# The order of the opening rearranged, and transposed probabilities as the weights of the value products

## The reference, cut to what matters

```python
def _L0_xattn_ref(q, k, v, mask, Wq, Wk, Wv, Wo):      # q = layernorm(x), k = v = ctx
    scores = jnp.einsum('bhqd,bhkd->bhqk', qh, kh) / scale
    scores = jnp.where(mask, NEG_INF, scores)
    attn = jax.nn.softmax(scores, axis=-1)
    ctx = jnp.einsum('bhqk,bhkd->bhqd', attn, vh)      # the value products
    return ctx.transpose(0, 2, 1, 3).reshape(B, S, D) @ Wo.T
x = x + _L0_xattn_ref(...)
# _L0_ffn_ref: logits -> top_k(2) -> softmax of the two = weights of the two experts
x = x + _L0_ffn_ref(_layernorm(x), ...)
```

## Time and profile before

| | |
|---|---|
| median of 3 runs | 192.21 us |
| the profiled execution | 192.32 us |
| its span | 190.5 us |
| granted clock of TensorE, mean | 0.991 of full |
| busy shares: TensorE, VectorE, ScalarE, GpSimd | 91%, 85%, 68%, 47% |

### The profile page before, as it was taken

One profiled execution on the slowest core, in us unless ns is written; L12 is line 12 of the kernel. 1 busy time (PEld: TensorE's weight loads), 2 busy tenths in 40 slices (PEclk: granted clock), 3 DMA queues, 4 the chain that ended last, 5 costly groups with the idle time before them and its releaser, 6 DMA issues.

```text
span 190.5 us, 4273 instructions
## 1 busy us (share of the span) xinstructions
PE 173.7 (91%) x1305; PEld 125.4 (66%) x1305; DVE 161.5 (85%) x505; ACT 129.8 (68%) x288; POOL 89.4 (47%) x146
## 2 busy tenths in 40 slices
PE   7888888879699999999899889999999999999962
PEld 7763555445556666666658566778887887887841
DVE  5577989999689998999994799987989798989981
ACT  3195897778569989999788855566555656565641
POOL 7059993595968888888778790500000000000000
PEclk9999999999889999999999999999999999999999
DMA  5999100000000000000000533232345235323301
GB/s 112 305 326 392 60 2 2 3 0 0 5 0 2 3 0 0 0 0 3 2 0 19 170 105 110 110 126 92 122 122 173 80 128 167 115 90 121 116 2 55
DMA packets 12128, 15.43 MB, mean 81 GB/s; under 512 B 1744, under 2 KB 6608, under 8 KB 11984
## 3 DMA queue, kind: packets, MB, share of 16 engines
q1 hardware_dynamic: 10800, 13.79, 22.1%
q10 hardware_dynamic: 1312, 1.46, 2.8%
HBM read 14.06 MB, written 1.18 MB: 80 GB/s over the span
## 4 chain that ended last, share of the span: by engine, by line
PE 53%; DVE 19%; POOL 7%; issue 7%; ACT 6%; DMA 4%; ACTq 1%; DVEq 0%; POOLq 0%
PE bank L1093 30%; PE bank L1040 8%; PE bank L1031 4%; DMA mhalf<-mask_half 4%; PE bank L1022 4%; DVE hid L905 4%; DVE smax L828 4%; DVE prob L849 3%; POOL k_blk L453 3%; ACT hid_hi L660 2%; PE bank L1011 2%; PE bank L1001 2%; POOL rstd L427 1%; DVE hid_lo L897 1%; PE bank L991 1%
## 5 line engine op out<-in xcount | busy, mean ns | idle before, releaser
L1040 PE MATMUL bank<-k_blk,q_blk 128*128 128x512 f32 x64 | 34.8, 629 | 1.1 <-POOL k_blk L453 0.9
L651 ACT ACTIVATE sig<-bank 128x512 f32<-128x512 f32 x36 | 21.5, 599 | 19.6 <-PE bank L1093 18.5
L453 POOL TENSOR_TENSOR k_blk<-k_all,consts_sb 128x512 f32<-128x512 f32 x32 | 33.1, 1056 | 0.0
L660 ACT CAST hid_hi<-hid 128x512 fp32r<-128x512 f32 (+1 forms) x37 | 22.4, 608 | 11.4 <-DVE hid L905 11.3
L1093 PE MATMUL bank<-xt_hi,w_hi 128*128 (+1 forms) x72 | 29.2, 406 | 0.2 <-ACT sig L651 0.2
L1093 PE MATMUL bank<-xt_hi,w_lo 128*128 (+1 forms) x72 | 28.3, 393 | 0.0
L1093 PE MATMUL bank<-xt_lo,w_hi 128*128 (+1 forms) x72 | 28.2, 392 | 0.0
L897 DVE TENSOR_TENSOR hid_lo<-hid,hid_hi 128x512 fp32r<-128x512 f32 (+1 forms) x37 | 25.1, 679 | 3.7 <-ACT hid_hi L660 3.3
L600 ACT ACTIVATE prob<-prob,exp_scale 128x512 f32<-128x512 f32 x32 | 23.8, 743 | 2.5 <-DVE prob L849 2.5
L888 DVE TENSOR_TENSOR hid_u<-sig,bank 128x512 f32<-128x512 f32 x32 | 21.8, 682 | 4.1 <-PE bank L1093 2.5
L828 DVE TENSOR_REDUCE smax<-bank 128x8 f32<-128x512 f32 x32 | 21.9, 684 | 2.8 <-PE bank L1040 2.8
(11 more groups left out here) (117 smaller groups left out, 333.7 us busy)
## 6 DMA issues: line engine op xcount, KB each, us to landing
cb<-comb_rows SPq DMA_DIRECT2D x64, 128.0 KB, 2.9
w_moe_sb<-w_moe SPq DMA_DIRECT2D x1, 1296.0 KB, 10.7
ctxt_sb<-ctx_t SPq DMA_DIRECT2D x4, 256.0 KB, 8.7
xt_sb<-x_t ACTq DMA_DIRECT2D x4, 256.0 KB, 7.7
x_sb<-x SPq DMA_DIRECT2D x4, 256.0 KB, 10.3
out<-x_sb SPq DMA_DIRECT2D x3, 256.0 KB, 3.1
w_moe_sb<-w_moe SPq DMA_DIRECT2D x1, 432.0 KB, 8.0
w_att_sb<-w_att SPq DMA_DIRECT2D x1, 264.0 KB, 4.7
```

Of the source, the lines that this page charges most:

```text
L453: last = nc.gpsimd.tensor_tensor(k_blk[p][:, g, :, :], k_all[:, bass.ds(t, 1), g, :].broadcast_to([P, HG, S]), hmask_sb.rearrange("p (h o) ...
L651: nc.scalar.activation(sig[r][:, :], gate_ps[r][:, :], ACT.Silu).then_inc(s_sig, 1)
L660: nc.scalar.copy(hid_hi[k][:, cols], hid[k][:, cols]).then_inc(s_hid_hi, 1)
L1040: nc.tensor.matmul(score_ps[g][:, :], q_blk[q][:, g, :, :].rearrange("p b s -> p (b s)"), k_blk[q][:, g, :, :].rearrange("p h s -> p (h s) ...
```

## The change

1. The probabilities become the weights: each of the 16 products of a tile loads 128 keys by 64 queries of `prob_t` as weights and moves 18 columns of `v_blk`. Batch `b` of every pair stands in the strip of columns `64 * b`, so there are two strips of 64 columns in place of four of 32. The output has queries on partitions, so `values_as_rows`, the copy to `pvt_sb` and their semaphores go, and VectorE reads the products' own output. `v_blk` shrinks from 32 to 18 columns for a pair, and the two memsets that zeroed its rest go. The copy that fills `v_blk` gets a wait for the products that read the buffer before.
2. VectorE's `norm1(1)` moves ahead of step -1, `keys(2)` from step 0 to step -1, `norm1(2)` from step 1 to step 0, `keys(3)` from step 2 to step 1, `norm1(3)` from step 3 to step 2. GpSimd's `rstd1_of(2)` moves from step 2 to step 1, `rstd1_of(3)` from step 3 to step 2.
3. The two operations of `weights_of_two` move from VectorE to ScalarE, behind the tanh.

```diff
@@ -121,8 +120,7 @@
 
         q_blk = [sb(f"q_blk{p}", [P, 2, BPT, S]) for p in range(2)]
         k_blk = [sb(f"k_blk{p}", [P, 2, HG, S]) for p in range(2)]
-        v_blk = [sb(f"v_blk{p}", [P, BPT, PAIRS, PW]) for p in range(2)]
-        pvt_sb = sb("pvt_sb", [P, 2 * P])
+        v_blk = [sb(f"v_blk{p}", [P, BPT, PAIRS, 2 * DV]) for p in range(2)]
         smax = [sb(f"smax{p}", [P, HEADS]) for p in range(2)]
         prob = [sb(f"prob{p}", [P, HEADS * S]) for p in range(2)]
         prob_t = [sb(f"prob_t{p}", [P, PAIRS, P]) for p in range(2)]
@@ -269,8 +265,7 @@
 
         score_ps = banks[5:7]
         pt_ps = [banks[7], banks[0]]
-        pvt_ps = banks[1][:, 0:2 * P]
-        pv_ps = banks[1][:, 2 * P:]
+        pv_ps = banks[1][:, 0:PAIRS * 2 * DV]
         at_ps, wo_ps, tail_ps = (bank[:, 0:P] for bank in banks[2:5])
 
         gate_ps = [banks[5], banks[7]]
@@ -346,6 +341,7 @@
 
             tiles = slice(half * TILES // 2, (half + 1) * TILES // 2)
             eng.wait_ge(s_w_top, half + 1)
+            eng.wait_ge(s_marked, half + 1)
             for k, dst in ((0, comb[half]), (1, comb_b[half])):
                 last = ops.tensor_tensor(dst[:, :, :], dst[:, :, :],
                                          w_top[:, tiles, k].rearrange("p (o t) -> p o t", o=1)
@@ -413,9 +409,6 @@
             nc.gpsimd.memset(neg_half[:, :], -0.5).then_inc(s_half, 1)
             nc.gpsimd.memset(eps_sb[:, :], LN_EPS).then_inc(s_half, 1)
             nc.gpsimd.memset(neg_mean_sb[:, :], -1.0 / D).then_inc(s_half, 1)
-            for p in range(2):
-                nc.gpsimd.memset(v_blk[p][:, :, :, :].rearrange("p b j w -> p (b j w)"), 0.0).then_inc(s_vwide, 1)
-
             nc.gpsimd.memset(v_all[:, TILES // 2:, :, :, :, :].rearrange("p t b j e d -> p (t b j e d)"), 0.0)\
                 .then_inc(s_zero[1], 1)
             pool.wait_ge(s_half, 4)
@@ -494,8 +487,8 @@
                     nc.gpsimd.tensor_tensor(bias2[p][:, :], neg_mean2[p][:, :], rstd2[p][:, :], ALU.mult).then_inc(s_bias2, 1)
                 if on(-2):
                     k_blocks(t + 2, p)
-                    if isinstance(t, int) and t in (0, 2, TRAIL):
-                        rstd1_of(1 + (t + 1) // 2)
+                    if isinstance(t, int) and t < GROUPS - 1:
+                        rstd1_of(t + 1)
                     if isinstance(t, int) and t == TRAIL:
                         pool.wait_ge(s_q_sb, GROUPS)
                         pool.wait_ge(s_k_sb, GROUPS)
@@ -576,13 +569,14 @@
                     act.wait_ge(s_wmoe[1], 16)
                 if on(-1):
                     if isinstance(t, int) and t < 0:
-                        act.wait_ge(s_vwide, 2)
                         act.wait_ge(s_vden, 2)
                         act.wait_ge(s_v_sb, 1)
                     elif isinstance(t, int) and t == 0:
                         act.wait_ge(s_v_sb, GROUPS)
 
-                    nc.scalar.copy(v_blk[q][:, :, :, 0:2 * DV].rearrange("p b j w -> p (b j) w"),
+                    if not (isinstance(t, int) and t < 1):
+                        act.wait_ge(s_pv, t)
+                    nc.scalar.copy(v_blk[q][:, :, :, :].rearrange("p b j w -> p (b j) w"),
                                    v_all[:, bass.ds(t + 1, 1), :, :, :, :].rearrange("p o b j e d -> p (o b j) (e d)"))\
                         .then_inc(s_vblk, 1)
                 if on(0):
@@ -618,9 +612,6 @@
                     nc.scalar.copy(xt2_hi[:, cols], tail_ps[:, 0:P]).then_inc(s_xt2_hi, 1)
                 if on(-1):
                     exponentials(0)
-                if on(0):
-                    act.wait_ge(s_pvt, t + 1)
-                    nc.scalar.copy(pvt_sb[:, :], pvt_ps).then_inc(s_pvt_sb, 1)
                 if on(-1):
                     exponentials(1)
 
@@ -633,6 +624,11 @@
                 tiles = slice(half * TILES // 2, (half + 1) * TILES // 2)
                 act.wait_ge(s_top_f, (half + 1) * TILES // 2)
                 nc.scalar.activation(half_tanh[:, tiles], gap[:, tiles], ACT.Tanh, scale=0.5).then_inc(s_tanh, 1)
+                act.wait_ge(s_tanh, half + 1)
+                for k, sign in ((0, -0.5), (1, 0.5)):
+                    last = nc.scalar.activation(w_top[:, tiles, k], half_tanh[:, tiles], ACT.Identity, scale=sign,
+                                                bias=half_sb[:, 0:1])
+                last.then_inc(s_w_top, 1)
 
             for g in range(GROUPS):
                 queries_out(g)
@@ -766,7 +762,6 @@
 
             def top_two(half):
                 experts_marked(half)
-                weights_of_two(half)
 
             def experts_marked(half):
 
@@ -775,17 +770,10 @@
                 iota_bc = iota_sb.rearrange("p (e o) -> p e o", o=1).broadcast_to(shape)
                 dve.wait_ge(s_top_f, (half + 1) * TILES // 2)
                 for k, dst in ((0, comb[half]), (1, comb_b[half])):
-                    nc.vector.tensor_tensor(dst[:, :, :], iota_bc,
-                                            top_f[:, tiles, k].rearrange("p (o t) -> p o t", o=1).broadcast_to(shape),
-                                            ALU.is_equal)
-
-            def weights_of_two(half):
-
-                tiles = slice(half * TILES // 2, (half + 1) * TILES // 2)
-                dve.wait_ge(s_tanh, half + 1)
-                for k, sign in ((0, -0.5), (1, 0.5)):
-                    last = nc.vector.tensor_scalar(w_top[:, tiles, k], half_tanh[:, tiles], sign, 0.5, ALU.mult, ALU.add)
-                last.then_inc(s_w_top, 1)
+                    last = nc.vector.tensor_tensor(
+                        dst[:, :, :], iota_bc, top_f[:, tiles, k].rearrange("p (o t) -> p o t", o=1).broadcast_to(shape),
+                        ALU.is_equal)
+                last.then_inc(s_marked, 1)
 
             def step(t, p, on):
                 q = 1 - p
@@ -832,7 +820,7 @@
                 if on(-1):
                     row_max(0)
                 if on(1):
-                    pv = pv_ps.rearrange("p (j w) -> p j w", w=PW)[:, :, 0:2 * DV].rearrange("p j (e d) -> p j e d", e=2)
+                    pv = pv_ps.rearrange("p (j e d) -> p j e d", e=2, d=DV)
                     dve.wait_ge(s_pv, t)
                     nc.vector.reciprocal(inv_den[q][:, :].rearrange("p (j e) -> p j e", e=2), pv[:, :, :, DK]).then_inc(s_iden, 1)
                     dve.wait_ge(s_iden, t)
@@ -853,16 +841,15 @@
                             ALU.subtract).then_inc(s_sub[g], 1)
                 if isinstance(t, int) and t == LEAD:
                     keys(1)
-                    norm1(1, 1)
-                if isinstance(t, int) and 0 <= t <= TRAIL:
-                    g = 2 + t // 2
-                    if t % 2 == 0:
-                        keys(g)
-                    else:
-                        norm1(g, g % 2)
+                    keys(2)
+                if isinstance(t, int) and t == 0:
+                    norm1(2, 0)
+                if isinstance(t, int) and t == 1:
+                    keys(3)
+                if isinstance(t, int) and t == 2:
+                    norm1(3, 1)
                 if isinstance(t, int) and t == TILES - 4:
                     experts_marked(0)
-                    weights_of_two(0)
                 if isinstance(t, int) and t == TILES - 3:
                     combined(dve, nc.vector, 0, s_route[0])
 
@@ -870,6 +857,7 @@
             share_rows(2)
             share_rows(3)
             norm1(0, 0)
+            norm1(1, 1)
             peel(step, LEAD)
             dve.wait_ge(s_bias, 16)
 
@@ -984,13 +972,6 @@
                     last = nc.tensor.matmul(v_ps[:, i * P:(i + 1) * P], ctxt_sb[:, c:c + P], wv_sb, start=True, stop=True)
                 last.then_inc(s_v, 1)
 
-            def values_as_rows(t):
-
-                pe.wait_ge(s_pvt_sb, t + 1)
-                for g in range(2):
-                    last = nc.tensor.transpose(pv_ps[:, g * P:(g + 1) * P], pvt_sb[:, g * P:(g + 1) * P], ident_sb)
-                last.then_inc(s_pv, 1)
-
             def attention_transposed(t, p):
                 pe.wait_ge(s_att, t + 1)
                 nc.tensor.transpose(at_ps, att[p][:, :, :].rearrange("p h d -> p (h d)"), ident_sb).then_inc(s_at, 1)
@@ -1029,8 +1010,10 @@
                         j = h * GT + c
                         for b in range(BPT):
                             last = nc.tensor.matmul(
-                                pvt_ps[c * PW:(c + 1) * PW, h * P + b * S:h * P + (b + 1) * S], v_blk[p][:, b, j, :],
-                                prob_t[p][:, j, b * S:(b + 1) * S], start=True, stop=True, tile_position=(0, c * PW))
+                                pv_ps[b * S:(b + 1) * S, j * 2 * DV:(j + 1) * 2 * DV],
+                                prob_t[p][:, j, b * S:(b + 1) * S],
+                                v_blk[p][:, b, j, :],
+                                start=True, stop=True)
                     return last
 
                 def scores(g):
@@ -1048,12 +1031,10 @@
                     pe.wait_ge(s_sub[0], TILES)
```

(13 more changed lines are left out.)

5 lines of the change are left out of this document (1 added, 4 removed).

## The result

| | before | changed |
|---|---|---|
| median, us | 191.87 (190.25 to 194.24, 20 runs) | 193.08 (191.73 to 196.15, 20 runs) |
| ratio to before | | 1.0066, 95% interval 1.0036 to 1.0096 |
| profiled execution, us (span) | 192.32 (190.5) | 196.15 (194.0) |
| mean granted clock, profiled | 0.991 | 0.970 |

The change makes the kernel slower by 0.7%. I had forecast 192.0 and no difference. The profiled execution of the changed kernel is its longest, and the ratio leaves out the five longest runs of the changed kernel and the three longest of the kernel before.

A forecast was written before the change was run, and what follows sets the result against it. Two tied circles bound a step at 4.52 us: TensorE's queue, and logits through `att` and value products to the router. Terms -2.0 + 2.2 - 0.45 - 0.1 = -0.35 against the profiled 192.32 gave 192.0 us, range 188.8 to 197.0.

The forecast's parts named there:

- The value products, +0.31 a tile: Value products on TensorE: weight loads bound them, 1.03 us a tile for 0.72, making loop steps 4.83 for 4.52.
- The sum over steps 5 to 11: Loop steps 5 to 11: seven circles, each longer by 0.31 us for the value products, +2.2 us.
- the rule that I had weighed: TensorE's value products: loads overlap running products only in other row groups; as a rival 194.2 us, chance 0.07.
- The opening, -2.0: Steps -1 to 4: moving norms and 1/sqrt earlier removes GpSimd's wait at the loop's entry, -2.0 us.
- 0.25 - (7.09 - 4.83): Opening: step 3 some 0.25 us later, step 4 falling from 7.09 to 4.83 if the clock stays; -2.0 us.
- Rival 1: Opening: half clock comes all the same, 193.4 us, chance 0.25; with an opening that gives nothing, 194.0, another 0.10.
- Step 12, -0.45: Step 12: VectorE loses the two weight operations to ScalarE, -0.45 us, between 0 and -0.57.
- costed the experts at nothing: Experts after the steps: TensorE's queue alone, unchanged; ScalarE's two operations, up to 0.2 us, paid by VectorE's freed 0.5.
- The end of the steps, -0.1: After the last step: without the `pvt_sb` copy ScalarE's table load starts earlier, part lost to lateness, -0.1 us.

The follow-up runs named there:

- the filled kernel: The changed kernel plus short products of constants in TensorE's waits of steps 2 and 3 and at the end: 191.82 us, ratio 1.0024 to before.
- `values_only`: The kernel before with only the change's value products, without `pvt_sb` and its transposes, old order kept: 194.11 us, ratio 1.0164.
- `wtop_only`: The kernel before with only the two operations on `w_top` moved to ScalarE: 190.83 us beside 190.78, ratio 0.9979.
- the filled kernels: Order alone, changed kernel and four strips, each with short constant products in TensorE's waits of steps 2 and 3 and at the end: 189.22, 191.82, 188.55 us.
- the order alone: The kernel before with everything of the change but the value products: 189.85 us, ratio 0.9925; with TensorE's waits filled 189.22.
- the four strips: The changed kernel with each value product cut in two, 32 queries as weights in four strips of 32 columns: 188.74 us, ratio 0.9878; filled 188.55.

## Why the prediction was wrong, point by point

**The value products, +0.31 a tile: right.** 1.04 forecast as 1.03, steps of 4.83, 0.52 of waiting, 0.2 us of idle TensorE ahead of the transpose of `att` (the second score product starts at 65.97 and takes 0.43, the transpose comes at 66.61). The sum over steps 5 to 11, forecast as +2.2, is 29.04 + 4.77 = 33.81 us now and 31.96 before, +1.9: step 7 had been 4.81 already. Loads 0.058 us apart in a strip with 64 columns go on beside that strip's products, as the trace has them. By the rule that I had weighed (the Trainium skill, TensorE: Matmul & The Clock Gate, Packing small matmuls), they would have waited for them, as the row group is the same; the measurement decides against it here.

**The opening, -2.0: this step failed**, in its term 0.25 - (7.09 - 4.83). The step of 4.83 came out where the clock stayed: 4.85 in the filled kernel, behind a step 3 of 6.05 for 5.91 (+0.14; 0.25 was forecast). What failed is the 7.09 and the condition "if the clock stays". At full clock the old order's step 4 is 5.92, with the new products in it (`values_only`), so the same term would have given 0.25 - (5.92 - 4.83) = -0.8; most of the rest of the -2.0 was clock. Without it the whole opening gains about 1.0: 34.28 us from the first row maximum to that of step 5, for an estimate of 35.3 (next paragraph).

The term added two things that do not belong together. One was real: the order shortens the way to step 5. With the new products on both sides and no half clock it is 34.28 us from the first row maximum to that of step 5 (filled) for 35.50 (`values_only`), -1.2. With the old products the changed order has 33.64 us (filled); for the old order no trace has it without half clock, and an estimate is 36.68 less the 1.4 that 3.41 us of half clock cost, 35.3: about -1.6. (The old order shows such a price too: `wtop_only`, with 3.41 us more of half clock than before, takes 1.46 us more over steps 3 to 5.) The other was the half clock itself. I read it in one profiled execution, called its disappearance a gain and set the sum against that execution. But it is not a property of the order. Of the kernel before, about half the runs have it: of the 17 beside the filled kernels 8 end between 190.3 and 191.0, with a mean clock of 0.998 to 1.00, and 9 between 191.4 and 193.0, with 0.988 to 0.993. The changed kernel has it more often: 17 of its 26 runs end above 192.5, and 13 have a mean clock of 0.978 or less, which 4 of the 51 runs of the kernel before beside the experiments have (part of that clock is lost at the end of the kernel). My 192.0 is in truth the time of the changed kernel where the clock stays: 191.82 with the waits filled.

**Rival 1 came true**, at the price given for it: "the clock falls in the opening all the same", 193.4, with 0.25. Measured 193.08. That the two agree to 0.3 is partly luck: the price was for 3.4 us of half clock in each execution, and the median lies between runs at 191.7 to 192.3 with little or none of it and runs at 192.9 to 196.15 with up to 6.8 us in the opening and more at the end. What should have raised its chance stood in the same text: the wait of 1 us only changes its place, from step 4 to step 3. What I held against it, that products lie closer around the wait, may be what keeps the clock in the profiled opening of the order alone; no run tests that. In the changed kernel the value products moving 18 columns take the place of those moving 64, right behind the wait. That alone does not explain why it falls more often: the four strips move 18 columns as well and have no `pvt_sb` either, and 4 of their 6 runs keep the clock. Why it falls in one execution and not in the next is open. Shown is that with the waits filled the fall was absent from the opening in every trace, and the times that went with it too.

**Step 12, -0.45: right in its place, wrong in the sum.** The step lost 0.55, and the way behind the last row maximum took back 0.50 (`wtop_only`), 0.36 of it among the last 18 units of the experts. I had costed the experts at nothing because TensorE's queue is full there; the pause is VectorE's, and TensorE waits for it: its next product of `hid_hi` starts at 144.97, right behind the end of `hid_lo` at 144.91.

**The end of the steps, -0.1: a gain that came larger and was not kept.** From the last tile's row maximum to the experts' first sigmoid it is 8.61 for 9.16 us. But the second group's first sigmoid is as late as before (29.47 for 29.42 from that row maximum), so what was gained is lost again before the loop. The last 4.9 to 6.0 us of the kernel can also be at half clock, a cost that the sum did not have; with the order alone the way from the last sigmoid to the end took 9.98 us with it and, the waits filled, 9.18.

The sum by these terms, for executions in which the clock stays while TensorE works: opening -1.6, +0.6 for the products in it (34.28 for 33.64), steps 5 to 11 +1.9, step 12 -0.55, from the last row maximum to the end +0.4 (94.27 for 93.8): +0.75 us. Measured so: 191.82 against a mean of 190.7 of the 8 undisturbed runs of before, +1.1; some 0.3 is not placed; the first row maximum alone moves by more than that from trace to trace (17.3 to 18.5). The order alone, by the same terms -1.6 - 0.55 + 0.5 = -1.6, was measured at 189.22 - 190.7 = -1.5, which bears out the estimate of -1.6. The falls then add 1.3 to the median of the changed kernel (193.08) and 1.2 to that of before (191.87): the medians differ by 1.2 as well. The forecast was -0.2, because it took some 1.4 us of clock from the one and left it out of the other.

## What to carry to other kernels

A stretch of half clock in a profile of before belongs to an execution, not to the kernel: compare with the spread and the clock of all runs before booking its absence as a gain, and set the sum against an execution without it. When a change moves a wait of TensorE near a stretch of half clock, fill the wait with cheap products and measure that as well, since it costs a few lines and separates the clock from the rest. And if swapping weights and moving data makes loads the bound, try more and narrower strips: here twice the instructions with half the weight columns were 3.3 us faster than the wide ones and 0.7 faster than the old orientation, all with their waits filled.

## What the runs showed of the hardware

- With products that move 18 columns, one strip of 32 or 64 float32 weight columns takes a load every 0.031 or 0.058 us beside running products of the same rows, and the four or two strips take theirs at the same time, 0.007 us apart.
- The same kernel with the same waits got half clock for 6.83 us in one execution and 3.41 in another, in one place, and none in four whose mean clock was 1.00. Each 3.41 us of it there cost 1.35 to 1.5.
- VectorE stood for 0.34 us in the experts' loop in all ten traces in which two instructions elsewhere in its list had moved to ScalarE, with all done that the trace shows it waiting for. What held it is open.
